# A Mamba scan's inputs: from VectorE and GpSimd to TensorE, with a diagonal that GpSimd selects

## The chip, the cores and the metric

The kernel runs on one core of one Trainium2 chip. The time is that of one launch in microseconds (us) on the device; times of several launches are given by their median. The profile is of one execution; its span runs from the first to the last instruction.

## The reference, cut to what matters

The whole program is four layers, each with an attention-like part and a feed-forward part. The change lies in the first layer's Mamba block, in its scan over time. The input is one sequence of 2048 tokens with 128 features; the block works on 256 channels and 16 states. The kernel takes the tokens in 4 blocks of 512 and the channels as 2 halves (j) of 128 partitions.

```python
dt = softplus(dt_r @ W_dt + b_dt)
A = -exp(A_log)
def step(h, ins):                       # over the 2048 tokens
    dt_t, B_t, C_t, u_t = ins
    dA = exp(dt_t[..., None] * A)
    h = h * dA + (dt_t * u_t)[..., None] * B_t[:, None, :]
    y = einsum('bds,bs->bd', h, C_t)
    return h, y
y = ys + uc * Dskip
```

For one state s, the scan over 512 tokens of a channel needs the factors exp(dt A[s]), the inputs (dt u) B[s], and then h C[s] is summed over s.

## The kernel before, in words

The scan is 64 steps, written out by hand. Step n has token block n // 16 and state n % 16. In each step:

- ScalarE makes the factors (`forget`, L586), one activation for each half j. They go to a PSUM bank (`decay(n, j)`, four banks, chosen by the parity of n and by j) or, in a step of kind T, to one of two SBUF buffers (`kept`).
- Some engine makes the inputs (dt u) B[s]. The string `KIND` says which, one letter for each step.
  - P: GpSimd multiplies `DTU` by a row of B that a DMA has spread over the partitions (`input_of`, L721), into `h(n)`.
  - D: TensorE spreads the row of B into PSUM (`spread`, L381) and VectorE multiplies (L840).
  - T: `DTU` was turned once for each block (`turn_dtu`, L406, kept by ScalarE, L597). Now tokens are the partitions and B[s] is a scalar for each partition, so ScalarE weights the turned copy with four activations (`weight`, L607, into `buT`), and TensorE turns it back into the `decay` bank with eight transposes (`turn_input`, L415).
- VectorE scans each half (`scan`, L860, 128x512), in place into `h(n)`, one of a ring of 5 buffers.
- GpSimd multiplies `h(n)` by the spread row of C (`read_out`, L731, 128x1024) into `hc`, a ring of 3.
- TensorE adds `hc` into the sum y with eight transposing matmuls (`add_y`, L435).

The order on each engine is a loop over n. TensorE issues the input of step n + 2, then now and then `turn_dtu`, `spread` or `turn_gated`, then `add_y(n - 1)`. ScalarE issues `weight(n + 3)`, then `forget(n + 2)`. GpSimd issues `read_out(n)`, then `input_of(n + 3)`. VectorE issues the two scans and, between them or behind them, what else it has. An input of step n by TensorE has to wait until the scan of step n - 2 has read the bank.

The step sizes dt of blocks 2 and 3 are finished during the scan of block 0. ScalarE computes exponentials at n = 1 and 4 and the logarithms at n = 8 (with its tables loaded anew, L566 and L586). VectorE then does `power_series` (L816), `soften` (L821), `add_soft` (L826: `DT` += the logarithm's part) and `scaled_u` (L830: `DTU` = `DT` u). At n = 2, 18, 34 and so on (from the second block on) it also gates the finished block (`gate`, L872, two instructions). At the start of each block `add_y` adds the diagonal of Dskip as well, with sixteen float32 matmuls that are no transposes (L428).

Before: 39 steps of kind T, 20 of kind P, 5 of kind D.

## Time and profile before

| what | us |
|---|---|
| median of 3 runs | 662.57 |
| lowest and highest of them | 659.83, 668.09 |
| the profiled execution, span | 632.2 |
| VectorE busy in it | 452.7 |
| TensorE (matmul) busy in it | 537.4 |
| ScalarE busy in it | 393.8 |
| GpSimd busy in it | 377.5 |
| the scan: start of its first instruction on VectorE, end of its last scan | 66.4, 250.0 |

For the profiled execution the span is what is recorded; a launch's time also holds what lies before and behind the span, and the median is 30.4 us above it. In the profile PE is TensorE's matmuls, PEld its weight loads, DVE VectorE, ACT ScalarE, POOL GpSimd, and L860 is line 860 of the kernel.

### The profile page before, as it was taken

What the parts mean: (1) busy time and instruction counts of PE and PEld (TensorE: products, weight loads), DVE (VectorE), ACT (ScalarE), POOL (GpSimd) and SP (SyncE); (2) the same over time, 40 slices, a digit from 0 to 9 for tenths busy, and PEclk for the clock granted to TensorE, in tenths of its full rate; (3) what the DMA queues carried; (4) which work ended last, traced back from release to release, by engine and by line L of the source; (5) the groups of instructions that cost most, each with busy time, mean ns of one, the idle gap of its engine ahead of it and who ended that gap; (6) DMA issues with size and microseconds to landing.
All of it is one profiled execution on the core that took longest, in us unless ns stands there. A gap on an engine that the chain in (4) does not pass through costs nothing. (4 is left out here: it accounts for less than half of the span.)

```text
span 632.2 us, 10057 instructions
## 1 busy us (share of the span) xinstructions
PE 537.4 (85%) x3490; PEld 423.8 (67%) x3490; DVE 452.7 (72%) x801; ACT 393.8 (62%) x779; POOL 377.5 (60%) x296
## 2 busy tenths in 40 slices
PE   5999867587787878798787989698999988989997
PEld 2444556466675767576654867698788986775766
DVE  6799799999999998898385597153333575658662
ACT  3679899769979987455469496413221135748670
POOL 0588798989999996488540650772900771125430
PEclk9999788799899899999999799899999999999999
DMA  5036053345666640200070000610611210000002
GB/s 131 4 84 108 16 122 101 83 113 130 134 139 131 135 121 2 76 0 2 17 210 3 1 8 28 147 64 17 183 32 45 66 34 2 2 0 1 2 0 67
DMA packets 45819, 40.44 MB, mean 64 GB/s; under 512 B 12183, under 2 KB 32585, under 8 KB 45770
## 3 DMA queue, kind: packets, MB, share of 16 engines
q1 hardware_dynamic: 44746, 37.71, 25.2%
q0 software_dynamic: 1024, 2.10, 1.1%
q8 instruction: 28, 0.46, 0.3%
q14 instruction: 21, 0.17, 0.1%
HBM read 33.70 MB, written 6.09 MB: 63 GB/s over the span
## 5 line engine op out<-in xcount | busy, mean ns | idle before, releaser
L435 PE MATMUL bank<-all_ident,l0s_ring 128*128 128x128 f32 x512 | 72.9, 291 | 18.7 <-POOL l0s_ring L731 18.5
L435 PEld LDWEIGHTS bank<-all_ident,l0s_ring 128*128 128x128 f32 x512 | 61.8, 150 | 27.4 <-POOL l0s_ring L731 24.8
L860 DVE TENSOR_TENSOR_SCAN l0s_ring<-l_XM,l0s_ring,bank 128x512 f32<-128x512 f32 x62 | 74.6, 1254 | 1.8 <-PE bank L415 1.8
L731 POOL TENSOR_TENSOR l0s_ring<-l0s_ring,l0s_c_rest 128x1024 f32<-128x1024 f32 x32 | 66.3, 2092 | 7.9 <-DVE l0s_ring L860 3.6
L731 POOL TENSOR_TENSOR l0s_ring<-l0s_ring,all_XF 128x1024 f32<-128x1024 f32 x31 | 66.2, 2154 | 5.8 <-DVE l0s_ring L860 2.7
L415 PE MATMUL bank<-all_ident,all_XNT 128*128 128x128 f32 x312 | 50.0, 302 | 22.9 <-DVE l0s_ring L860 15.7
L607 ACT ACTIVATE all_XNT<-l_wraw,l_wins 128x256 f32<-128x256 f32 x156 | 66.1, 497 | 0.5 <-PE bank L415 0.4
L860 DVE TENSOR_TENSOR_SCAN l0s_ring<-bank,l0s_ring 128x512 f32<-128x512 f32 x50 | 60.2, 1244 | 5.1 <-ACT bank L586 2.5
L415 PEld LDWEIGHTS bank<-all_ident,all_XNT 128*128 128x128 f32 x312 | 39.3, 156 | 29.7 <-ACT all_XNT L607 12.7
L586 ACT ACTIVATE l_XM<-l_DT,l_negA 128x512 f32<-128x512 f32 x78 | 50.8, 712 | 0.6 <-DVE l0s_ring L860 0.6
L721 POOL TENSOR_TENSOR l0s_ring<-l_DTU,l0s_b_all 128x1024 f32<-128x1024 f32 x20 | 40.1, 2005 | 0.0
L586 ACT ACTIVATE bank<-l_DT,l_negA 128x512 f32<-128x512 f32 x50 | 32.7, 679 | 7.0 <-DVE l0s_ring L860 7.0
L2015 POOL DMA_INDIRECT all_XNT<-gy,all_slot x16 | 15.6, 974 | 35.9 <-DMA gy<-l1s_ys 31.6
L329 PE MATMUL bank<-l_XM,l_wins 128*128 128x512 f32 x64 | 30.9, 627 | 0.9 <-ACT l_XM L530 0.9
L1386 POOL TENSOR_TENSOR l1m_prep<-l1at_NWT,l1at_level 128x512 f32<-128x512 f32 x12 | 15.9, 1351 | 22.8 <-issue 20.5
L2027 POOL TENSOR_TENSOR l1s_xlo<-all_XF,l1s_xhi 128x512 fp32r<-128x512 f32 x7 | 7.7, 1094 | 32.4 <-ACT l1s_xhi L2474 32.4
L2887 PEld LDWEIGHTS bank<-l_w,l_wall 128*128 128x128 f32 x128 | 19.0, 226 | 8.5 <-issue 5.7
L2448 ACT ACTIVATE l1s_U<-bank 128x128 f32<-128x128 f32 x16 | 4.4, 277 | 32.4 <-PE bank L2108 32.4
L329 PEld LDWEIGHTS bank<-l_XM,l_wins 128*128 128x128 f32 x64 | 12.1, 200 | 16.8 <-issue 15.5
L2327 PE MATMUL bank<-all_wdT,l1s_work 128*128 128x128 f32 x192 | 22.8, 275 | 0.0
L2887 PE MATMUL bank<-l_w,l_wall 128*128 128x128 f32 x128 | 19.8, 315 | 3.3 <-ACT l_wall L2895 2.0
L2676 DVE SCALAR_TENSOR_TENSOR l1s_work<-bank,l_wall 128x512 f32<-128x512 f32 x24 | 15.9, 683 | 9.2 <-ACT l_wall L2480 7.3
(442 smaller groups left out, 1497.7 us busy)
## 6 DMA issues: line engine op xcount, KB each, us to landing
l0s_c_rest<-bc_rows SPq DMA_DIRECT2D x16, 512.0 KB, 5.4
all_XF<-bc_rows SPq DMA_DIRECT2D x16, 512.0 KB, 5.3
l0s_b_all<-bc_rows SPq DMA_DIRECT2D x20, 256.0 KB, 6.0
l_wall<-in_L_ffn_W SPq DMA_DIRECT2D x14, 256.0 KB, 4.7
all_X<-in_L_attn_x SPq DMA_DIRECT2D x4, 256.0 KB, 3.5
gx<-l1m_TD SPq DMA_DIRECT2D x1, 1024.0 KB, 5.6
gy<-l1m_TD SPq DMA_DIRECT2D x1, 1024.0 KB, 8.6
out<-all_X SPq DMA_DIRECT2D x4, 256.0 KB, 2.3
```

The lines of the kernel that those rows point to most:

```text
L329: last = nc.tensor.matmul(S.bank[j][:, :], wins[:, k, j * P:(j + 1) * P], XM[:, b * BLK + k:b * BLK + k + BLK], start=(k == 0), stop=(k == ...
L415: last = nc.tensor.transpose(decay(n, j)[:, bass.ts(k, P)], buT[i % 2][:, k, j * P:(j + 1) * P], S.ident[:, :])
L435: last = nc.tensor.matmul(y_of(k, j), hc[n % CRING][:, j, bass.ts(k, P)], S.ident[:, :], start=False, stop=(n % DS == DS - 1 and k % 2 == ...
L586: nc.scalar.activation(dst, DT[:, j, block_of(n)], ACT.Exp, scale=negA[:, j, n % DS:n % DS + 1]).then_inc(decay_ready, 1)
L607: last = nc.scalar.activation(buT[i % 2][:, k, :], dtuT[:, k, :], ACT.Identity, scale=bT[:, n // DS * TPB + k, DR + n % DS:DR + n % DS + 1])
L721: nc.gpsimd.tensor_tensor(h(n)[:, :, :], DTU[:, :, block_of(n)], wide(b_wide[i % HRING]), ALU.mult).then_inc(bu_pool, 1)
L731: nc.gpsimd.tensor_tensor(hc[n % CRING][:, :, :], h(n)[:, :, :], wide(c_wide[p % HRING][:, n % 2, :]), ALU.mult).then_inc(hc_ready, 1)
L860: nc.vector.tensor_tensor_scan(h(n)[:, j, :], factor, added, before, ALU.mult, ALU.add).then_inc(h_ready, 1)
L1386: nc.gpsimd.tensor_tensor(LL[:, LEVELS - 1 - l, q, :, :], LT[:, quads(q), :], quad(level[:, l, :]), ALU.mult).then_inc(ll_ready, 1)
L2327: last = nc.tensor.matmul(out_bank[:, bass.ts(k, P)], hid[b % 2][:, f, bass.ts(k, P)], wdT[:, f, :], start=(b >= NBLK and f == 0 and k == ...
L2676: nc.vector.scalar_tensor_tensor(hid[b % 2][:, f, :], up_bank[n][:, :], QSCALE, sg[n % 2], ALU.mult, ALU.mult).then_inc(hid_done, 1)
L2887: last = self.nc.tensor.matmul(out, self.hid[b % 2][:, f, bass.ts(k, P)], self.E.down(0)[:, f, :], start=(f == 0), stop=(f == FE - 1))
```

## The change

- There is a new kind of step, G. GpSimd makes a diagonal matrix of B[s] for each of a block's four tiles of 128 tokens in one instruction (`diagonal`, an affine select on 128x512 that keeps the element where column equals partition and writes zero elsewhere), and TensorE multiplies the turned dt u by it (`spread_input`, eight float32 matmuls of 128x128 that are no transposes). This turns back and weights at once, and ScalarE has nothing to weight. 26 steps are G, 34 T, 2 P and 2 D.
- Both kinds keep their factors in the two `kept` buffers, so `forget(n)` of all steps from the fourth on waits for the scan of step n - 2.
- The turned dt u has two buffers, chosen by the block's parity, the second in `OUTF`, whose first use there (`q_of[2]`) must be over: `keep_dtu(1)` waits for `dt_ready` 3.
- `add_soft` and `scaled_u` of blocks 2 and 3 move from VectorE to GpSimd, one step earlier in the loop: behind `read_out` at n = 10 and 13, and n = 11 and 14.

The diff, without the lines that declare the semaphore `diag_ready`:

```diff
--- before.py
+++ after.py
@@ -184,9 +184,11 @@
         STEPS = NBLK * DS
         EXP_AT, LOG_AT = (1, 4), 8
         TURN_AT, ROWS_AT = (4, 6), (STEPS - 7, STEPS - 5, STEPS - 3, STEPS - 1)
-        KIND = "DPDPTPTTPTTPTTPT" + (NBLK - 2) * "PTTPTTPTDTPTTPTT" + "PTTPTTPTDTPTTTTT"
+        KIND = "DPDPTGGTGGTGTTTT" + "TTGTGTGTGTTGTGTG" + 2 * "TGTGTTGTGTGTTGTG"
         LAST = STEPS - 1
         number = lambda n: KIND[:n].count(KIND[n])
+        by_pe = [n for n in range(STEPS) if KIND[n] in "TG"]
+        turns = lambda n: sum(m < n for m in by_pe)
         BC = DR + DS
         GROUP = [slice(0, TPB), slice(TPB, TILES)]
         with Phase(nc, "l0s") as ph:
@@ -215,8 +217,9 @@
 
             buT = [S.XNT[:, i * 2 * TPB:(i + 1) * 2 * TPB, :].rearrange("p (k j) d -> p k (j d)", j=JT) for i in range(2)]
             kept = [XM[:, i * W2:(i + 1) * W2].rearrange("p (j t) -> p j t", j=JT) for i in range(2)]
-            dtuT = wraw[:, 0:W2].rearrange("p (k c) -> p k c", k=TPB)
+            dtuT = [v[:, 0:W2].rearrange("p (k c) -> p k c", k=TPB) for v in (wraw, S.OUTF)]
             bT = wins[:, :, :].rearrange("p k d -> p (k d)")[:, 0:TILES * BC].rearrange("p (n c) -> p n c", c=BC)
+            diagB = [v.rearrange("p (k t) -> p k t", k=TPB) for v in (win[:, :], wins[:, :, :].rearrange("p k d -> p (k d)")[:, BLK:2 * BLK])]
             nw = (6 * P + FF0) // Q16
             wa, wc = (ring[:, PADS + 3 * SPOT + i * nw * Q16:PADS + 3 * SPOT + (i + 1) * nw * Q16].rearrange("p (n q) -> p n q", q=Q16) for i in range(2))
             nq = TPB * P // Q16
@@ -413,6 +416,17 @@
                             pe.wait_ge(h_ready, JT * (n - 2) + j + 1)
                             for k in range(TPB):
                                 last = nc.tensor.transpose(decay(n, j)[:, bass.ts(k, P)], buT[i % 2][:, k, j * P:(j + 1) * P], S.ident[:, :])
+                            last.then_inc(bu_turned, 1)
+
+                    def spread_input(n):
+                        i = number(n)
+                        pe.wait_ge(diag_ready, i + 1)
+                        pe.wait_ge(dtu_kept, 2 * (n // DS + 1))
+                        for j in range(JT):
+                            pe.wait_ge(h_ready, JT * (n - 2) + j + 1)
+                            for k in range(TPB):
+                                last = nc.tensor.matmul(decay(n, j)[:, bass.ts(k, P)], dtuT[n // DS % 2][:, k, j * P:(j + 1) * P], diagB[i % 2][:, k, :],
+                                                        start=True, stop=True)
                             last.then_inc(bu_turned, 1)
 
                     def add_y(n):
@@ -488,6 +502,8 @@
                     for n in range(STEPS + 1):
                         if n + 2 < STEPS and KIND[n + 2] == "T":
                             turn_input(n + 2)
+                        if n + 2 < STEPS and KIND[n + 2] == "G":
+                            spread_input(n + 2)
                         if n + 6 < STEPS and (n + 6) % DS == 0:
                             turn_dtu((n + 6) // DS, 0)
                             turn_dtu((n + 6) // DS, 1)
@@ -574,15 +590,15 @@
                             nc.scalar.activation(wdT[0:96, 2, :], S.bank[5][0:96, 2 * P:3 * P], ACT.Copy).then_inc(w_copied, 1)
 
                     def forget(n, j):
-                        if KIND[n] == "T":
-                            i = number(n)
+                        if KIND[n] in "TG":
+                            i = turns(n)
                             if i >= 2:
-                                act.wait_ge(h_ready, JT * [m for m in range(n) if KIND[m] == "T"][i - 2] + j + 1)
+                                act.wait_ge(h_ready, JT * by_pe[i - 2] + j + 1)
                         elif n >= 2:
                             act.wait_ge(h_ready, JT * (n - 2) + j + 1)
                         if n % DS == 0 and j == 0:
                             act.wait_ge(dt_ready, n // DS + 1)
-                        dst = kept[number(n) % 2][:, j, :] if KIND[n] == "T" else decay(n, j)[:, :]
+                        dst = kept[turns(n) % 2][:, j, :] if KIND[n] in "TG" else decay(n, j)[:, :]
                         nc.scalar.activation(dst, DT[:, j, block_of(n)], ACT.Exp, scale=negA[:, j, n % DS:n % DS + 1]).then_inc(decay_ready, 1)
 
                     def keep_b():
@@ -590,21 +606,23 @@
                         nc.scalar.activation(bT, bank_t[:, 0:TILES * BC].rearrange("p (n c) -> p n c", c=BC), ACT.Copy).then_inc(b_kept, 1)
 
                     def keep_dtu(b):
-                        if b:
-                            act.wait_ge(weighted, KIND[:b * DS].count("T"))
+                        if b == 1:
+                            act.wait_ge(dt_ready, 3)
+                        elif b:
+                            act.wait_ge(bu_turned, JT * turns((b - 1) * DS))
                         for i in range(2):
                             act.wait_ge(dtu_turned, 2 * b + i + 1)
-                            nc.scalar.activation(dtuT[:, 2 * i:2 * i + 2, :], (bank_b if i else bank_t)[:, :].rearrange("p (k c) -> p k c", k=2),
+                            nc.scalar.activation(dtuT[b % 2][:, 2 * i:2 * i + 2, :], (bank_b if i else bank_t)[:, :].rearrange("p (k c) -> p k c", k=2),
                                                  ACT.Copy).then_inc(dtu_kept, 1)
 
                     def weight(n):
                         i = number(n)
                         if i >= 2:
-                            act.wait_ge(bu_turned, JT * (i - 1))
+                            act.wait_ge(bu_turned, JT * (turns([m for m in by_pe if KIND[m] == "T"][i - 2]) + 1))
                         act.wait_ge(b_kept, 1)
                         act.wait_ge(dtu_kept, 2 * (n // DS + 1))
                         for k in range(TPB):
-                            last = nc.scalar.activation(buT[i % 2][:, k, :], dtuT[:, k, :], ACT.Identity,
+                            last = nc.scalar.activation(buT[i % 2][:, k, :], dtuT[n // DS % 2][:, k, :], ACT.Identity,
                                                         scale=bT[:, n // DS * TPB + k, DR + n % DS:DR + n % DS + 1])
                         last.then_inc(weighted, 1)
 
@@ -730,6 +748,26 @@
                             pool.wait_ge(y_added, n - CRING + 1)
                         nc.gpsimd.tensor_tensor(hc[n % CRING][:, :, :], h(n)[:, :, :], wide(c_wide[p % HRING][:, n % 2, :]), ALU.mult).then_inc(hc_ready, 1)
 
+                    def diagonal(n):
+                        i = number(n)
+                        pool.wait_ge(b_kept, 1)
+                        if i >= 2:
+                            pool.wait_ge(bu_turned, JT * (turns([m for m in by_pe if KIND[m] == "G"][i - 2]) + 1))
+                        else:
+                            pool.wait_ge(z_ready, 2 * NBLK)
+                        row = bT[:, n // DS * TPB:(n // DS + 1) * TPB, DR + n % DS:DR + n % DS + 1]
+                        nc.gpsimd.affine_select(out=diagB[i % 2], in_=row.broadcast_to([P, TPB, P]), compare_op=ALU.is_equal, fill=0.0, base=0,
+                                                pattern=[[0, TPB], [1, P]], channel_multiplier=-1).then_inc(diag_ready, 1)
+
+                    def add_soft(b):
+                        pool.wait_ge(softened, b + 1)
+                        pool.wait_ge(max_ready, JT * (b + 1))
+                        nc.gpsimd.tensor_tensor(DT[:, :, blk(b)], DT[:, :, blk(b)], q_of[b], ALU.add).then_inc(dt_ready, 1)
+
+                    def scaled_late(b):
+                        pool.wait_ge(dt_ready, b + 1)
+                        nc.gpsimd.tensor_tensor(DTU[:, :, blk(b)], DT[:, :, blk(b)], UC[:, :, blk(b)], ALU.mult).then_inc(dtu_late, 1)
+
                     nc.gpsimd.memset(wraw[96:P, 2 * P:3 * P], 0.0).then_inc(zeroed, 1)
                     nc.gpsimd.memset(wraw[96:P, 5 * P:6 * P], 0.0).then_inc(zeroed, 1)
                     pool.wait_ge(zeroed, 2)
@@ -759,6 +797,12 @@
                             read_out(n)
                         if n + 3 < STEPS and KIND[n + 3] == "P":
                             input_of(n + 3)
+                        if n + 3 < STEPS and KIND[n + 3] == "G":
+                            diagonal(n + 3)
+                        if n in (10, 13):
+                            add_soft(2 if n == 10 else 3)
+                        if n in (11, 14):
+                            scaled_late(2 if n == 11 else 3)
 
                 @block.vector
                 def _(dve):
@@ -825,10 +869,6 @@
                         dve.wait_ge(max_ready, JT * (b + 1))
                         nc.vector.tensor_tensor(DT[:, :, blk(b)], DT[:, :, blk(b)], q_of[b], ALU.add).then_inc(dt_ready, 1)
 
-                    def scaled_u(b):
-                        dve.wait_ge(dt_ready, b + 1)
-                        nc.vector.tensor_tensor(DTU[:, :, blk(b)], DT[:, :, blk(b)], UC[:, :, blk(b)], ALU.mult).then_inc(dtu_late, 1)
-
                     def input_of(n):
                         dve.wait_ge(b_spread, number(n) + 1)
                         if n // DS < 2:
@@ -846,7 +886,7 @@
                         elif KIND[n] == "D":
                             dve.wait_ge(bu_dve, i + 1)
                         else:
-                            dve.wait_ge(bu_turned, JT * i + j + 1)
+                            dve.wait_ge(bu_turned, JT * turns(n) + j + 1)
                             if n == 4:
                                 dve.wait_ge(wq_ready, 1)
                             if n >= RING:
@@ -855,8 +895,8 @@
                         if n >= DS:
                             dve.wait_ge(h_ready, JT * (n - DS) + j + 1)
                         before = h(n - DS)[:, j, BLK - 1:BLK] if n >= DS else 0.0
-                        factor = kept[i % 2][:, j, :] if KIND[n] == "T" else decay(n, j)[:, :]
-                        added = decay(n, j)[:, :] if KIND[n] == "T" else h(n)[:, j, :]
+                        factor = kept[turns(n) % 2][:, j, :] if KIND[n] in "TG" else decay(n, j)[:, :]
+                        added = decay(n, j)[:, :] if KIND[n] in "TG" else h(n)[:, j, :]
                         nc.vector.tensor_tensor_scan(h(n)[:, j, :], factor, added, before, ALU.mult, ALU.add).then_inc(h_ready, 1)
 
                     def read_last():
@@ -922,10 +962,6 @@
                             power_series(2 if n == 3 else 3)
                         if n in (10, 13):
                             soften(2 if n == 10 else 3)
-                        if n in (11, 14):
-                            add_soft(2 if n == 11 else 3)
-                        if n in (12, 15):
-                            scaled_u(2 if n == 12 else 3)
                         if n >= DS and n % DS == 2:
                             gate(n // DS - 1)
                     read_last()
```

## Rows read from the trace of the kernel before

**Rows 1.** The page: the span, and VectorE's busy tenths in 40 slices

```profile
span 632.2 us, 10057 instructions
...
DVE  6799799999999998898385597153333575658662
```

**Rows 2.** Windows, one for each quarter of the scan: busy us (instructions) of each engine, clock, DMA

```profile
66.30:124.96 58.66, 39.74 (x240) 34.09 (x240) 54.79 (x45) 53.31 (x96) 50.16 (x23) 0.79 0.35 86
124.96:166.19 41.23, 32.36 (x243) 27.50 (x241) 40.22 (x37) 34.93 (x71) 39.28 (x21) 0.96 0.54 123
166.19:207.56 41.37, 32.40 (x243) 27.95 (x242) 40.17 (x36) 37.83 (x77) 41.13 (x22) 0.96 0.64 134
207.56:250.00 42.44, 34.14 (x262) 30.07 (x262) 40.38 (x35) 36.25 (x73) 39.29 (x20) 0.96 0.39 87
```

**Rows 3.** Groups by line and shape, VectorE, 66 to 254 us: busy, mean ns | idle before

```profile
L860 DVE TENSOR_TENSOR_SCAN l0s_ring<-l_XM,l0s_ring,bank 128x512 f32<-128x512 f32 x62 | 74.6, 1254 | 1.8 <-PE bank L415 1.8
L860 DVE TENSOR_TENSOR_SCAN l0s_ring<-bank,l0s_ring 128x512 f32<-128x512 f32 x50 | 60.2, 1244 | 5.1 <-ACT bank L586 2.5 <-POOL l0s_ring L721 2.4
L860 DVE TENSOR_TENSOR_SCAN l0s_ring<-l_XM,bank 128x512 f32<-128x512 f32 x16 | 18.4, 1196 | 0.4 <-ACT l_XM L586 0.4
L840 DVE TENSOR_TENSOR l0s_ring<-l_DTU,bank 128x1024 f32<-128x1024 f32 x5 | 6.0, 1200 | 3.0 <-PE bank L381 3.0
...
L830 DVE TENSOR_TENSOR l_DTU<-l_DT,l_UC 128x1024 f32<-128x1024 f32 x2 | 3.9, 1965 | 0.0
L826 DVE TENSOR_TENSOR l_DT<-l_DT,all_OUTF 128x1024 f32<-128x1024 f32 x2 | 3.9, 1964 | 0.0
```

**Rows 4.** Timeline of VectorE: start, us, instructions, idle before and its releaser

```profile
105.07 2.34 DVE L860 TENSOR_TENSOR_SCAN l0s_ring<-bank,l0s_ring 128x512 f32<-128x512 f32 x2 [1.55 <-ACT bank L586]
107.33 1.20 DVE L826 TENSOR_TENSOR l_DT<-l_DT,all_OUTF 128x1024 f32<-128x1024 f32 x1
...
118.95 2.73 DVE L826 TENSOR_TENSOR l_DT<-l_DT,all_OUTF 128x1024 f32<-128x1024 f32 x1
...
127.33 4.76 DVE L860 TENSOR_TENSOR_SCAN l0s_ring<-l_XM,l0s_ring,bank 128x512 f32<-128x512 f32 x4
132.01 1.25 DVE L872 TENSOR_TENSOR l_ZT<-bank,l_ZT 128x512 f32<-128x512 f32 x2
...
239.09 2.45 DVE L860 TENSOR_TENSOR_SCAN l0s_ring<-l_XM,l0s_ring,bank 128x512 f32<-128x512 f32 x2 [0.55 <-PE bank L415]
```

**Rows 5.** Timeline of GpSimd in the scan

```profile
63.14 2.35 POOL L708 TENSOR_TENSOR l_DTU<-l_DT,l_UC 128x1024 f32<-128x1024 f32 x1
...
90.80 2.98 POOL L731 TENSOR_TENSOR l0s_ring<-l0s_ring,all_XF 128x1024 f32<-128x1024 f32 x1
...
233.21 7.88 POOL L731 TENSOR_TENSOR l0s_ring<-l0s_ring,l0s_c_rest 128x1024 f32<-128x1024 f32 x4
```

**Rows 6.** Timeline of GpSimd in the next layer, where it selects on 128x512

```profile
361.83 0.63 POOL L1381 TENSOR_SCALAR_AFFINE_SELECT l1at_DEC<-l1at_DEC 128x512 f32<-128x512 f32 x1 [2.02 <-ACT l1at_DEC L1606]
...
364.85 1.05 POOL L1381 TENSOR_SCALAR_AFFINE_SELECT l1at_DEC<-l1at_DEC 128x512 f32<-128x512 f32 x1 [1.37 <-ACT l1at_DEC L1606]
```

**Rows 7.** Timeline of TensorE: two stretches of the scan

```profile
133.32 2.05 PE L428 MATMUL bank<-l_diagD,l_UC 128*128 128x128 f32 x16 [0.52 <-DVE l_ZT L872]
135.21 1.91 PE L435 MATMUL bank<-all_ident,l0s_ring 128*128 128x128 f32 x16
```

**Rows 8.** Timeline of TensorE in a stretch at the lower clock

```profile
85.49 1.82 PE L435 MATMUL bank<-all_ident,l0s_ring 128*128 128x128 f32 x8
```

**Rows 9.** Window of that stretch

```profile
83.70:87.10 3.40, 3.40 (x16) 3.17 (x17) 3.05 (x3) 3.40 (x8) 2.66 (x3) 0.50 0.29 98
```

**Rows 10.** Timeline of ScalarE behind its two logarithms

```profile
102.98 1.28 ACT L586 ACT_TABLE_LOAD   x1
...
105.52 1.69 ACT L607 ACTIVATE all_XNT<-l_wraw,l_wins 128x256 f32<-128x256 f32 x4
107.12 2.54 ACT L586 ACTIVATE l_XM<-l_DT,l_negA 128x512 f32<-128x512 f32 x4
```

4 lines of the change are left out of this document (2 added, 2 removed).

## The prediction

> **What bounds the kernel now.** I read the page first, for where VectorE's tenths stay at nines [rows 1]: from slice 4 to 15, the scan. Then the windows over its four blocks [rows 2]. VectorE is busy 54.8 of 58.7 us in the first, and 40.2, 40.2 and 40.4 of 41.2, 41.4 and 42.4 in the others. GpSimd comes close behind it (50.2, 39.3, 41.1, 39.3), ScalarE and TensorE lie lower. Scans are serial on VectorE: 128 of them at 1.20 to 1.25 us [rows 3]. So VectorE's queue is the path, and what counts is what leaves it and what can't keep up with it afterwards. The groups by line [rows 3] show both at once: busy time of each thing that VectorE does, and its idle time with the releaser. Beyond the scan nothing reads what the change moves, so a gain there passes to the end undiminished.
>
> Back to back, four scans take 4.68 us (start 127.33 to the gate at 132.01) [rows 4], 1.17 each, 2.34 a step; the gate takes 1.2. A block of 16 steps thus costs VectorE 37.4 + 1.2 = 38.7 us at least, against the 41.2 to 42.4 that it takes now. In the first block, whose scans start from zero (mean 1196 ns, not 1254 [rows 3]), I take 1.12 a scan and 2.24 a step.
>
> **What leaves VectorE.** Three of five D inputs at 1.20 (L840), two `add_soft` at 1.96 and two `scaled_u` at 1.97 [rows 3]: 3.6 + 3.9 + 3.9 = 11.4 us, all on the path. With them go two kinds of waits: for GpSimd's inputs (L721), 2.4 us, and for TensorE's turned inputs (L415), 1.8 us [rows 3]. The latter stand where KIND ends in five T steps: a T step costs ScalarE four weights and two factors, and its scans start late (0.55 idle at 239.09 [rows 4]). The new string has no such run at its end. Upper bound: 15.6 us.
>
> The moved operations are worth their means because of how they collide. `add_soft` took 1.20 us once and 2.73 the other time [rows 4], and a `read_out` beside such an operation took 2.98 in place of 1.97 [rows 5]. Both engines lose when VectorE has two operands in SBUF. A scan has one in SBUF and one in PSUM, so it doesn't disturb GpSimd. The Trainium skill, SBUF — State Buffer, "Who interferes with whom", states this as an exclusive lock on a shared port pair that a VectorE instruction with two SBUF inputs takes against a GpSimd instruction that reads SBUF. The trace agrees (2.73 against 1.20). By this rule no other sum comes out, but it says that the moved pair costs GpSimd no collision of its own.
>
> **What comes on GpSimd.** A `read_out` costs 1.97 (four in 7.88 [rows 5]), and so does an input. A moved operation costs 2.3, by its twin of the early blocks, 2.35 [rows 5]. The diagonal is not in the scan before. The next layer has the same instruction on the same shape: 0.63, or 1.05 beside VectorE instructions of another kind [rows 6]. The input here is a broadcast column, which no row shows for a select. I take 0.63, since only scans run beside it, and keep 1.05 for the range. A block behind the first has 16 read-outs and 7 diagonals: 31.5 + 4.4 = 35.9 us (38.9 by the high price) against VectorE's 38.7. GpSimd has room, or just none.
>
> A diagonal can also be late rather than too much. `diagonal(n + 3)` stands behind `read_out(n)`, which starts when scan n ends. 1.97 + 0.63, then four matmuls and their latency, 0.65: 3.3 us. The scan that needs it starts four scans later, 4.7. Slack 1.4 us (1.0 by the high price), so GpSimd may trail by about one microsecond before VectorE waits.
>
> At the end of the first block it trails by more. I count from the end of ScalarE's table load at 104.3 behind the logarithms [rows 10]. Scan 11 can end 2.9 later (half its factors 0.62, two scans). From there GpSimd has five read-outs (9.8), one of them stretched by 1.0 beside `soften`, and three of the moved operations (6.9), then the diagonal of step 18 (0.6) and the matmuls (0.65): 21.9 in all. VectorE would be at scan 18 at 20.6 (next paragraph). Cost 1.3 us, once; then GpSimd catches up 2.8 us a block.
>
> **What comes on ScalarE.** Five weights of 1.6 us fewer in all, so less work. But steps 12 to 17 are now all T, which makes 1.6 + 1.24 = 2.84 a step on ScalarE [rows 10] against 2.24 on VectorE; before, P steps stood among them and VectorE's moved work covered them. From the end of the table load: factors of 11 (1.24), five weights (8.0), the turned dt u of block 1 (1.05), factors of 12 to 15 (5.0) and half of 16 (0.6): scan 16 at 15.9. VectorE alone: 0.6 + 5 x 2.24 + 1.9 for `soften` = 13.7. Cost 2.2 us. Scan 16 stands at 124.96 now, 20.7 behind the same mark, so even so it comes 4.8 earlier. After it two T steps at 2.34 make the 20.6 above. The 1.55 us that VectorE waits at 105.07 for these tables [rows 4] shrink little. In later blocks T runs are two long. `keep_gated`, queued ahead of two factors, makes one step late by some 0.4 in each: 1 us for the three with jitter. That all factors now wait for the scan two steps back costs nothing while ScalarE is on time: 3 scans (3.5 us) lie between, for at most 2.84 of work.
>
> **What comes on TensorE.** 39 steps were its own, now 60. Sixteen float32 matmuls that are no transposes take 2.05, sixteen transposes 1.91 [rows 7]: 0.128 and 0.119 each at the full clock. A block: 16 `add_y` 15.3, 9 T 8.6, 7 G 7.2, the Dskip diagonal 2.05, turning dt u and the gated rows 2.9: 36.0 of 38.7 us. It fits, with 7% to spare, so I count nothing; the cover is the 1.4 us of slack. At the lower clock eight take 1.82 [rows 8], where the granted clock is 0.50, 1.2 GHz [rows 9]; a step then takes 3.64, 1.3 over VectorE's. The blocks behind the first had 0.96 on average [rows 2], one short stretch each, in which TensorE had been idle often. It will be idle less, so I expect no more of them.
>
> The Trainium skill speaks against the change here. FP8 and Floating Point Precision, "TensorE Precision Notes", has true float32 take four passes through the array, and TensorE: Matmul & The Clock Gate, "Terms", calls transpose mode four times faster for float32. By that rule each G step would cost four times the transposes' time; the row has 0.128 against 0.119, 8% more, on the same shape and kind of operands. I follow the row.
>
> **DMA.** 18 of 20 spreads of B (256 KB each) go; VectorE never waits for one, so nothing.
>
> **The sum.** 11.4 + 2.4 + 1.8 - 1.3 - 2.2 - 1.0 = 11.1 us off the scan. The profiled span would go from 632.2 to 621.1. What lies around it, 30.4 us between that span and the median of the runs, stays: 662.6 - 11.1 = 651.5, say 651, 1.7% less. A change under 2%, 13 us, is about what a measurement of this kernel can't tell from none.
>
> **The rivals.** (A) GpSimd becomes the second bound: diagonals cost 1.05 or more each, GpSimd needs 38.9 a block, and every run of G T G waits. For it: GpSimd was within 2 us of VectorE before, and a broadcast input is unseen. Against: 0.63 stands for the quiet case. Bound by GpSimd, the three blocks give back 0.2 each, and by late diagonals some 0.3 on 21 G steps: 6 to 7 us lost, 658. (B) The waits that I added don't come: ScalarE and GpSimd have enough run-up before step 12 and 18, since both lose work in the first ten steps. Then 15.6 of gain less 0.6: 647; and if the wait at 105.07 goes too, 645. (C) The other side: TensorE becomes the bound. Non-transposing matmuls in float32, or a busy engine that is stopped by late diagonals, put it at 1.2 GHz for long stretches. At 1.3 us a step it takes 9 such steps to eat the gain and 19 to be slower by 2%; at two of the three blocks, 32 steps, 651 + 42 = 693. By the page's four passes, worked out from the rows: a G step needs 8 x 4 x 0.119 + 0.95 = 4.8, 2.4 over VectorE's, on 26 steps 62 us: 713. Against both: [rows 7], and a clock of 0.96 on average with TensorE busy 32 of 41 us [rows 2]. That the change doesn't do what it says can be seen from the diff only for GpSimd's select, and would be (A).
>
> **How the numbers follow.** Forecast 0.55, with 646 to 656 as its own range; A 0.20; B 0.18; C 0.07 (clock 0.05, four passes 0.02). Forecast and B hold the faster side: all of B, and a third of the forecast's cases end under 649.3. Faster by over 2% 0.35, within 2% 0.58, slower 0.07. The range takes in B's low end, with a few microseconds for the spread of the runs (659.8 to 668.1), and A's high end: 642 to 662.
>
> **What would show it.** In the new profile: scan stage 66.4 to about 239 rather than 250; VectorE's blocks behind the first at 38.7 to 39.5 us; L826 and L830 as GpSimd groups at 2.3 each; selects at 0.63; VectorE's idle in front of scans released by ScalarE at steps 12 to 16, once by TensorE at 18; the L415-like group of G at 0.128 spacing. The prediction is wrong if VectorE waits on TensorE in every G step (A or C), if the granted clock falls under 0.9 behind the first block (C), or if GpSimd's read-outs stretch beside scans.

## The result: faster by 0.8%, less than half of what was forecast

Before 664.28 us (median of 20 runs), after 659.73 (20 runs). The ratio is 0.9922, 95% interval 0.9901 to 0.9944, so about 5 us or 0.8% faster, where 11.1 us were forecast. The direction is right; the size is not.

The traces need one remark. The first trace of before has a span of 632.2 us, 30 us under that kernel's median. A second trace of before (the run `null_before` below) has 664.5, and 31.3 of the 32.3 us between them lie behind the scan. The largest piece that I found is one wait of GpSimd at a phase's end, behind sixteen indirect DMAs: 11.9 us in the first trace, 26.6 in the second:

```profile
459.32 0.20 POOL L2041 MEMSET l1s_ST<- 128x128 f32 x1 [26.57 <-POOLq L63]
```

That run took 666.31 us for a span of 664.5, and after's profiled run 661.33 for 659.6. So only 1.8 us lie around the span, and not the 30.4 that the prediction put there. The record doesn't say which chip the first trace is from; on the chip of the last four experiments this kernel's spans were 632.6 to 641.8 us, so it is most likely one of that kind. The scan itself is nearly the same in both traces of before: 182.4 and 182.8 us from the start of the first scan to the end of the last. All sums below are made inside the scan.

Line numbers are those of each kernel, and they shift. In after L900 is a scan, L912 the gate, L418 the input of a T step, L428 that of a G step (in before L428 was the diagonal of Dskip, now L442), L449 `add_y`, L460 `turn_gated`, L602 a factor, L625 a weight, L632 `keep_gated`, L759 the new diagonal, L765 and L769 the two moved operations.

I cut the scan at the starts of steps 16, 32 and 48 on VectorE, by the starts of single scans in the traces:

| kernel | first block | second | third | fourth | scan, us |
|---|---|---|---|---|---|
| before (second trace) | 57.8 | 41.2 | 41.4 | 42.5 | 182.8 |
| after | 52.7 | 45.3 | 41.1 | 41.4 | 180.5 |
| forecast | 52.5 | 40.4 | 39.1 | 39.1 | about 171 |

The last row isn't in the prediction; I put it together from its parts. Scan 16 was to come 4.8 us earlier (57.3 in the first trace, less 4.8), the later blocks were to take 38.7 to 39.5 us, and 1.3 us of waiting at step 18 falls in the second. The first block came out as forecast, within 0.2 us; how far that was luck, the experiments show. The loss stands in the three others: 4.9, 2.0 and 2.3 us. VectorE's groups in after, to be read against [rows 3]:

```profile
L900 DVE TENSOR_TENSOR_SCAN l0s_ring<-l_XM,l0s_ring,bank 128x512 f32<-128x512 f32 x96 | 114.7, 1258 | 10.4 <-ACT l_XM L602 5.0 <-PE bank L428 3.0 <-PE bank L418 2.1
L900 DVE TENSOR_TENSOR_SCAN l0s_ring<-l_XM,bank 128x512 f32<-128x512 f32 x24 | 27.4, 1197 | 3.6 <-ACT l_XM L602 2.3 <-PE bank L418 1.4
L900 DVE TENSOR_TENSOR_SCAN l0s_ring<-bank,l0s_ring 128x512 f32<-128x512 f32 x8 | 9.3, 1207 | 1.6 <-ACT bank L602 1.5
```

L826 and L830 are gone from this view and L840 (now L880) has 2 instructions left. But the idle time ahead of scans is 15.6 us, where it was 1.8 + 5.1 + 0.4 = 7.3. The timeline of VectorE says where, against [rows 4]. Steps 11, 12, 15, 16 and 17, then 18, then around the gates (L912):

```profile
106.63 2.33 DVE L900 TENSOR_TENSOR_SCAN l0s_ring<-l_XM,bank 128x512 f32<-128x512 f32 x2 [2.25 <-ACT l_XM L602]
109.46 2.33 DVE L900 TENSOR_TENSOR_SCAN l0s_ring<-l_XM,bank 128x512 f32<-128x512 f32 x2 [0.49 <-PE bank L418]
...
119.11 2.33 DVE L900 TENSOR_TENSOR_SCAN l0s_ring<-l_XM,bank 128x512 f32<-128x512 f32 x2 [0.41 <-PE bank L418]
122.01 4.79 DVE L900 TENSOR_TENSOR_SCAN l0s_ring<-l_XM,l0s_ring,bank 128x512 f32<-128x512 f32 x4 [0.56 <-PE bank L418]
129.63 2.65 DVE L900 TENSOR_TENSOR_SCAN l0s_ring<-l_XM,l0s_ring,bank 128x512 f32<-128x512 f32 x2 [2.83 <-PE bank L428]
132.20 1.26 DVE L912 TENSOR_TENSOR l_ZT<-bank,l_ZT 128x512 f32<-128x512 f32 x2
...
144.78 2.45 DVE L900 TENSOR_TENSOR_SCAN l0s_ring<-l_XM,l0s_ring,bank 128x512 f32<-128x512 f32 x2 [1.16 <-ACT l_XM L602]
147.60 2.45 DVE L900 TENSOR_TENSOR_SCAN l0s_ring<-l_XM,l0s_ring,bank 128x512 f32<-128x512 f32 x2 [0.36 <-ACT l_XM L602]
150.91 23.54 DVE L900 TENSOR_TENSOR_SCAN l0s_ring<-l_XM,l0s_ring,bank 128x512 f32<-128x512 f32 x20 [0.85 <-PE bank L418]
174.37 1.25 DVE L912 TENSOR_TENSOR l_ZT<-bank,l_ZT 128x512 f32<-128x512 f32 x2
...
186.23 2.45 DVE L900 TENSOR_TENSOR_SCAN l0s_ring<-l_XM,l0s_ring,bank 128x512 f32<-128x512 f32 x2 [1.16 <-ACT l_XM L602]
189.05 7.30 DVE L900 TENSOR_TENSOR_SCAN l0s_ring<-l_XM,l0s_ring,bank 128x512 f32<-128x512 f32 x6 [0.37 <-ACT l_XM L602]
...
215.49 1.26 DVE L912 TENSOR_TENSOR l_ZT<-bank,l_ZT 128x512 f32<-128x512 f32 x2
```

These lines show three kinds of wait. At 106 the 2.25 is for ScalarE's factors behind its logarithms. From 109 to 122 the waits of 0.49 (twice), 0.41 and 0.56 come from ScalarE's run of T steps: they name TensorE, but TensorE itself had been waiting for ScalarE's weights (L625), as its line for step 15 shows:

```profile
118.42 1.09 PE L418 MATMUL bank<-all_ident,all_XNT 128*128 128x128 f32 x8 [1.90 <-ACT all_XNT L625]
```

At 129.63 step 18 waits 2.83 for TensorE's new line L428. Behind the gates a scan waits 1.16 for a factor of ScalarE, twelve microseconds after the gate, and the next one 0.37; this repeats at 186.23 and, not shown, at 227.35. From gate to gate it is 42.2 and 41.1 us.

GpSimd's new groups in after:

```profile
L759 POOL TENSOR_SCALAR_AFFINE_SELECT l_wins<-l_wins 128x512 f32<-128x512 f32 x13 | 9.3, 714 | 0.0
L759 POOL TENSOR_SCALAR_AFFINE_SELECT l_win<-l_wins 128x512 f32<-128x512 f32 x13 | 8.3, 638 | 0.0
L769 POOL TENSOR_TENSOR l_DTU<-l_DT,l_UC 128x1024 f32<-128x1024 f32 x2 | 4.7, 2364 | 0.0
L765 POOL TENSOR_TENSOR l_DT<-l_DT,all_OUTF 128x1024 f32<-128x1024 f32 x2 | 4.7, 2358 | 0.0
```

The select costs 0.64 (one took 1.62, beside a VectorE operation with two SBUF inputs), a moved operation 2.36. These prices were forecast well, 0.63 and 2.3. The select that step 18 needs comes late all the same, since it stands behind a read-out:

```profile
124.87 2.00 POOL L749 TENSOR_TENSOR l0s_ring<-l0s_ring,all_XF 128x1024 f32<-128x1024 f32 x1
126.82 0.64 POOL L759 TENSOR_SCALAR_AFFINE_SELECT l_wins<-l_wins 128x512 f32<-128x512 f32 x1
```

TensorE's prices were not forecast well. Its timeline in after at the first late diagonal and in the third block:

```profile
127.52 3.44 PE L428 MATMUL bank<-l_wins,all_OUTF 128*128 128x128 f32 x16 [3.77 <-POOL l_wins L759]
130.80 1.04 PE L449 MATMUL bank<-all_ident,l0s_ring 128*128 128x128 f32 x8
...
132.54 1.95 PE L428 MATMUL bank<-l_win,all_OUTF 128*128 128x128 f32 x16
```

```profile
183.31 1.04 PE L449 MATMUL bank<-all_ident,l0s_ring 128*128 128x128 f32 x8
184.18 0.60 PE L460 MATMUL bank<-all_ident,l_ZT 128*128 128x128 f32 x4
...
186.37 1.95 PE L428 MATMUL bank<-l_wins,l_wraw 128*128 128x128 f32 x16
```

A G step issues 16 MATMULs for its 8 calls, and takes 1.95 us, not 1.03. And the windows, one around the first line of that timeline and then the last three blocks, with the columns of [rows 2]:

```profile
127.50:130.90 3.40, 3.38 (x17) 3.38 (x18) 1.27 (x1) 1.78 (x5) 3.40 (x2) 0.56 0.77 137
...
122.00:167.30 45.30, 39.74 (x337) 38.31 (x335) 39.43 (x34) 36.42 (x72) 38.83 (x26) 0.96 0.34 89
167.40:208.40 41.00, 39.66 (x345) 37.90 (x344) 39.05 (x35) 36.30 (x73) 35.81 (x24) 1.00 0.46 103
208.50:249.80 41.30, 39.91 (x348) 38.20 (x347) 39.27 (x35) 33.39 (x65) 35.76 (x23) 1.00 0.33 73
```

TensorE is busy 39.7 of 41.0 us in the third block, where it was 32.4 of 41.4. It looks like the bound. Whether it is, the experiments had to say.

### The profile page after: what moved, and what is told of

Its sections match the earlier page's. It is cut to its first block and busy times, and to the rows that moved or that the text cites. A ratio compares the mean times of both kernels' runs of the same rounds, so it can differ in the third digit from the quotient of the medians.

```text
span 659.6 us, 10816 instructions
## 1 busy us (share of the span) xinstructions
PE 575.4 (87%) x3860; PEld 465.6 (71%) x3860; DVE 447.1 (68%) x794; ACT 386.9 (59%) x759; POOL 365.9 (55%) x308
## 5 line engine op out<-in xcount | busy, mean ns | idle before, releaser
L900 DVE TENSOR_TENSOR_SCAN l0s_ring<-l_XM,l0s_ring,bank 128x512 f32<-128x512 f32 x96 | 114.7, 1258 | 10.4 <-ACT l_XM L602 5.0
L602 ACT ACTIVATE l_XM<-l_DT,l_negA 128x512 f32<-128x512 f32 x120 | 79.1, 712 | 8.8 <-DVE l0s_ring L900 8.8
L449 PE MATMUL bank<-all_ident,l0s_ring 128*128 128x128 f32 x512 | 66.0, 273 | 0.3 <-POOL l0s_ring L749 0.3
L449 PEld LDWEIGHTS bank<-all_ident,l0s_ring 128*128 128x128 f32 x512 | 57.8, 141 | 0.7 <-POOL l0s_ring L749 0.7
L418 PE MATMUL bank<-all_ident,all_XNT 128*128 128x128 f32 x272 | 35.6, 274 | 6.1 <-ACT all_XNT L625 6.1
L418 PEld LDWEIGHTS bank<-all_ident,all_XNT 128*128 128x128 f32 x272 | 30.4, 141 | 7.6 <-ACT all_XNT L625 7.5
L2051 POOL DMA_INDIRECT all_XNT<-gy,all_slot x16 | 15.6, 976 | 35.5 <-DMA gy<-l1s_ys 31.2
L625 ACT ACTIVATE all_XNT<-all_OUTF,l_wins 128x256 f32<-128x256 f32 x72 | 30.5, 496 | 0.2
L900 DVE TENSOR_TENSOR_SCAN l0s_ring<-l_XM,bank 128x512 f32<-128x512 f32 x24 | 27.4, 1197 | 3.6 <-ACT l_XM L602 2.3
L2484 ACT ACTIVATE l1s_U<-bank 128x128 f32<-128x128 f32 x16 | 4.4, 277 | 40.5 <-PE bank L2144 32.1
L625 ACT ACTIVATE all_XNT<-l_wraw,l_wins 128x256 f32<-128x256 f32 x64 | 27.1, 496 | 0.2
L1607 PE MATMUL bank<-l1m_TD,l1m_prep 128*128 128x128 f32 x96 | 15.6, 320 | 13.1 <-DVE l1m_TD L1934 7.7
L1607 PEld LDWEIGHTS bank<-l1m_TD,l1m_prep 128*128 128x128 f32 x96 | 14.1, 228 | 14.3 <-issue 10.2
```

The source lines that it names most:

```text
L418: last = nc.tensor.transpose(decay(n, j)[:, bass.ts(k, P)], buT[i % 2][:, k, j * P:(j + 1) * P], S.ident[:, :])
L449: last = nc.tensor.matmul(y_of(k, j), hc[n % CRING][:, j, bass.ts(k, P)], S.ident[:, :], start=False, stop=(n % DS == DS - 1 and k % 2 == ...
L602: nc.scalar.activation(dst, DT[:, j, block_of(n)], ACT.Exp, scale=negA[:, j, n % DS:n % DS + 1]).then_inc(decay_ready, 1)
L625: last = nc.scalar.activation(buT[i % 2][:, k, :], dtuT[n // DS % 2][:, k, :], ACT.Identity, scale=bT[:, n // DS * TPB + k, DR + n % DS:DR ...
L900: nc.vector.tensor_tensor_scan(h(n)[:, j, :], factor, added, before, ALU.mult, ALU.add).then_inc(h_ready, 1)
L1607: last = nc.tensor.matmul(S.bank[2 * q][:, bass.ts(k, P)], LL[:, LEVELS - 1 - l, q, k, :], TD[:, q * TPB + k, :], start=True, stop=True)
```

## The experiments

Three theories. (1) TensorE's load: a G step costs nearly twice what I thought, and a block needs about 38.7 us of TensorE (an estimate from its lines), as much as of VectorE. (2) Late diagonals: their place behind `read_out` in GpSimd's queue. (3) The hand-over. After each gate TensorE turns the gated rows (`turn_gated`, L460) and ScalarE copies them out of the bank (`keep_gated`, L632). ScalarE works its queue in order, so while `keep_gated` waits for `turn_gated`, the two factors behind it wait too. Beside them the question what each half of the change does alone.

Ratios are to before on the same chip. The last four experiments, from first_gate on, ran on a chip where before takes 639.16 us, not 664. No trace of before was kept there; the first trace of before, which is as short, has a scan of 182.4 us, the second 182.8. `null_before` is before once more.

**null_before.** 

> The kernel before once more, for its spread and for a second trace. Ratio to before 1.000 with an interval of about 0.003 to either side. Its scan should again take 183 to 184 us on VectorE from its first input to its last scan; the time behind the scan is expected near 405 us, as in the trace of after, and not the 382 us of the first trace of before.

Ratio 0.9996 (0.9963 to 1.0028). Scan 182.8, behind it 413 us, 31 more than in the first trace. So differences of ratios under 0.003 mean nothing, and the blocks of the scan are the finer measure. Between the two traces of before the first block differs by 0.5 us, the others by 0.01, so 0.5 us of any whole scan below can be chance; each of the other kernels has but one trace.

**g_one_pass.** Theory 1 by itself: G's product in half the MATMULs. It leaves out the factor B of these steps, so only its time counts.

```diff
 for k in range(TPB):
-    last = nc.tensor.matmul(decay(n, j)[...], dtuT[n // DS % 2][...], diagB[i % 2][:, k, :], start=True, stop=True)
+    last = nc.tensor.transpose(decay(n, j)[...], dtuT[n // DS % 2][...], S.ident[:, :])
```

> After, with each G step's product done as eight transposes against the identity in place of eight float32 matmuls against the diagonal, which is still selected and waited for. The input of these steps is left without its factor B, so the output is another one. Theory 1 (TensorE is the second bound: in the trace of after a G step issues 16 MATMULs, two for each call, and costs 1.8 us, not 1.0, so that a block needs 38.7 us of TensorE, as much as of VectorE): a G step falls to 0.9 us, a block to 32.5 us of TensorE, the waits of VectorE behind each gate (0.3 to 1.2 us each, 1.5 to 2 us a block) mostly go, and the time falls by 4 to 6 us against after, ratio to before 0.984 to 0.987. Theory 2 (late diagonals and order on GpSimd): nothing but the wait at step 18 matters and it stays, within 1 us of after, ratio 0.991 to 0.994. Theory 3 (the hand-over of the gated rows from TensorE to ScalarE waits for its place in the order, whatever TensorE's load is): within 1.5 us of after.

Ratio 0.9906 (0.9872 to 0.9939). The ratio can't tell it from after, the scan can: 175.0, with blocks 52.1, 43.0, 39.9, 40.0. It is 5.5 us shorter than after, 5.0 without the first block. The wait at 18 is 1.9 in place of 2.8, the waits behind the gate of the third block 0.27 and 0.37 in place of 1.16 and 0.37. Theory 1 forecast 4 to 6 us and gets them in the scan, though not in the ratio (it had 0.984 to 0.987). But the larger waits only shrank, at the same steps; two small ones (0.34 and 0.22 at steps 21 and 22) went.

**diag_first.** Theory 2: the order on GpSimd.

```diff
 for n in range(STEPS):
+    if n + 3 < STEPS and KIND[n + 3] == "G":
+        diagonal(n + 3)
     if n < LAST:
         read_out(n)
-    if n + 3 < STEPS and KIND[n + 3] == "G":
-        diagonal(n + 3)
```

> After, with diagonal(n + 3) issued ahead of read_out(n) on GpSimd, not behind it. Theory 1 (TensorE): the 2.8 us wait of VectorE at step 18 shrinks to 1 us or less, since TensorE turns the input while GpSimd reads out, the waits behind the gates stay; 1 to 2.5 us faster than after, ratio 0.988 to 0.991. Theory 2 (late diagonals): the waits behind the gates go as well, 4 to 6 us faster than after, ratio 0.984 to 0.987. Theory 3: as theory 1.

Ratio 0.9839 (0.9785 to 0.9893). Scan 176.4, blocks 52.5, 42.5, 40.7, 40.8; 4.1 us off after, 2.8 of them in the second block. From step 16, which it waits for, VectorE goes through step 18 without a stop, up to the gate:

```profile
120.73 7.20 DVE L900 TENSOR_TENSOR_SCAN l0s_ring<-l_XM,l0s_ring,bank 128x512 f32<-128x512 f32 x6 [0.57 <-PE bank L418]
127.84 1.26 DVE L912 TENSOR_TENSOR l_ZT<-bank,l_ZT 128x512 f32<-128x512 f32 x2
```

TensorE's product of step 18 starts 3.55 us behind scan 16 and takes 2.05. In after it started 5.51 behind it, later by one read-out of 2.00, and took 3.44: TensorE had idled for 3.77 us, and the clock granted there was 0.56, near the lower of its two levels (the window above). So the late diagonal had been paid twice, once for the select's place and once for the clock. The waits behind the gates stayed (0.76 and 0.37 in the third block): theory 2 is a part, not the whole.

**inputs_only.** The change without the moved step sizes.

```diff
 # vector
 if n in (10, 13):
     soften(2 if n == 10 else 3)
+if n in (11, 14):
+    add_soft(2 if n == 11 else 3)
+if n in (12, 15):
+    scaled_u(2 if n == 12 else 3)
 # gpsimd
-if n in (10, 13):
-    add_soft(2 if n == 10 else 3)
-if n in (11, 14):
-    scaled_late(2 if n == 11 else 3)
```

> After, with add_soft and scaled_u of blocks 2 and 3 back on VectorE in their old places: the G and T inputs alone. Theory 1 (TensorE bounds the blocks behind the first): VectorE reaches step 16 some 4 us later, GpSimd is not behind then and the wait at step 18 (2.8 us) goes; later blocks stay at 41 us; 1 to 3 us slower than after, ratio 0.995 to 1.000. Rival (the moved step sizes carry the whole gain at 7.8 us of VectorE's queue): 5 us slower or more, ratio 1.000 or above.

Ratio 0.9888 (0.9844 to 0.9931). Scan 178.6, blocks 53.6, 42.5, 41.15, 41.4. Neither expectation: both had it slower than after, and its scan is 1.9 us shorter. Three of the four moved operations, back on VectorE in this kernel:

```profile
107.78 1.20 DVE L857 TENSOR_TENSOR l_DT<-l_DT,all_OUTF 128x1024 f32<-128x1024 f32 x1
111.14 1.20 DVE L861 TENSOR_TENSOR l_DTU<-l_DT,l_UC 128x1024 f32<-128x1024 f32 x1
117.85 1.20 DVE L857 TENSOR_TENSOR l_DT<-l_DT,all_OUTF 128x1024 f32<-128x1024 f32 x1
```

All four take 1.20, 4.8 us together, where before they took 1.20, 2.74, 2.73 and 1.20, 7.9 together. With GpSimd's P inputs gone, each of them starts ahead of GpSimd's read-out, which then takes 2.84 in place of 2.00; in before two of them started behind an instruction of GpSimd and took the longer time themselves. So 3.1 of the 7.8 us are saved by the new inputs, whether anything is moved or not; VectorE's other operations with two SBUF inputs in that block fall from 9.9 us (7.6 in the first trace of before, which waits 1.7 us more) to 7.1. That is how this kernel has 4.2 of the 5.1 us that after gains in the first block. Of the 4.8 us that the move takes off VectorE, 1.95 come back in after as the four waits for ScalarE's run of T steps, and 0.7 as a longer `soften` (1.93 for 1.20, beside a read-out): over steps 11 to 15, where the two kernels differ on VectorE, this kernel is only 1.4 us longer, over the whole first block 1.0. And the second block, where GpSimd isn't behind now, is 2.9 shorter.

**steps_only.** The other half alone: before with `add_soft` and `scaled_u` moved.

```diff
 # vector
-if n in (11, 14):
-    add_soft(2 if n == 11 else 3)
-if n in (12, 15):
-    scaled_u(2 if n == 12 else 3)
 # gpsimd
+if n in (10, 13):
+    add_soft(2 if n == 10 else 3)
+if n in (11, 14):
+    scaled_late(2 if n == 11 else 3)
```

> Before, with only add_soft and scaled_u of blocks 2 and 3 moved to GpSimd, as in after. Scan of before, first scan to last: 57.8 + 41.2 + 41.4 + 42.5 = 182.8 us by block. Theory A (moved steps pay what they took on VectorE): the first block falls by 5 to 7 us, the others stay, scan 176 to 178. Theory B (they only move the load from the first engine to the second, GpSimd, which then has 44 + 9 us against VectorE's 49): the first block falls by 3 to 5, the second rises by 1 to 3, scan 179 to 182.

Ratio 0.9992 (0.9970 to 1.0015): nothing. Scan 185.2, 2.4 longer than before: the first block 2.7 shorter, the second 4.8 longer. Both theories had a gain. B is right in its direction, the first block's gain taken back in the second, but the second loses more than it allowed (1 to 3), so that nothing is left. VectorE in the trace of this kernel, steps 16 and 18:

```profile
123.70 2.46 DVE L873 TENSOR_TENSOR_SCAN l0s_ring<-bank,l0s_ring 128x512 f32<-128x512 f32 x2 [3.64 <-POOL l0s_ring L721]
...
130.85 2.45 DVE L873 TENSOR_TENSOR_SCAN l0s_ring<-l_XM,l0s_ring,bank 128x512 f32<-128x512 f32 x2 [2.34 <-PE bank L415]
```

VectorE waits 3.64 us for GpSimd's input of step 16, which stands behind `scaled_u` and two read-outs, then 2.34 for a turned input.

**first_steps_dve.** diag_first and inputs_only together.

```diff
 # gpsimd
+if n + 3 < STEPS and KIND[n + 3] == "G":
+    diagonal(n + 3)
 if n < LAST:
     read_out(n)
-if n + 3 < STEPS and KIND[n + 3] == "G":
-    diagonal(n + 3)
-if n in (10, 13):
-    add_soft(2 if n == 10 else 3)
-if n in (11, 14):
-    scaled_late(2 if n == 11 else 3)
 # vector
+if n in (11, 14):
+    add_soft(2 if n == 11 else 3)
+if n in (12, 15):
+    scaled_u(2 if n == 12 else 3)
```

> Diagonals ahead of the read-outs and the late step sizes back on VectorE. If the moved steps cost 1.9 us in after (scan 180.5 against 178.6 without them) only because diagonals came late behind them, they are worth their first-block gain here: this scan is 0.5 to 1.5 us longer than that of diag_first, 177 to 178. Rival (they cost on their own, by GpSimd's lag): it is as short or shorter, 175 to 176.4.

Ratio 0.9830 (0.9798 to 0.9863). Scan 176.5, blocks 54.1, 41.0, 40.65, 40.75, against 176.4 for diag_first. With the moved operations back on VectorE the first block is 1.6 longer and the second 1.5 shorter. The result, 0.1 longer, lies between the two expectations (0.5 or more, or as short): even with diagonals first the moved operations are worth nothing.

**gate_later.** Theory 3: the hand-over, on after as it is.

```diff
-TURN_AT, ROWS_AT = (4, 6), ...
+TURN_AT, ROWS_AT = (4, 7), ...
 # scalar
-if n > DS and n % DS - 1 in TURN_AT:
-    keep_gated(n // DS - 1, TURN_AT.index(n % DS - 1))
+if n > DS and n % DS - 2 in TURN_AT:
+    keep_gated(n // DS - 1, TURN_AT.index(n % DS - 2))
```

> After, with ScalarE's keep_gated one step later (n % 16 = 6 and 9) and TensorE's second turn_gated one step later (n % 16 = 7), so that ScalarE does not wait at the head of its queue while two factors stand behind it. If the order of the hand-over makes the waits of 1.16 and 0.37 us behind each gate, blocks three and four fall from 41.1 and 41.4 to 39.5 to 40.0 and the scan to 176 to 177.5. If TensorE's load behind the gate makes them (it has no idle for 15 us there), the waits move to the scans that wait for TensorE and the blocks stay at 40.5 or more, scan 179 to 180.5.

Ratio 0.9829 (0.9799 to 0.9859). Scan 174.5, blocks 52.1, 43.1, 39.06, 40.3: 6.0 us off after (5.4 without the first block, which the edit doesn't touch), by moving three numbers, with the same work on every engine. That is more than the expectation had for theory 3 (176 to 177.5). This decides between theories 1 and 3 for the third block: all seven G steps are in it, TensorE does what it did, and the block takes 39.06, where theory 1 had 40.5 or more. Timeline of VectorE in it, gate to gate:

```profile
170.79 1.26 DVE L912 TENSOR_TENSOR l_ZT<-bank,l_ZT 128x512 f32<-128x512 f32 x2
171.97 9.54 DVE L900 TENSOR_TENSOR_SCAN l0s_ring<-l_XM,l0s_ring,bank 128x512 f32<-128x512 f32 x8
181.69 28.25 DVE L900 TENSOR_TENSOR_SCAN l0s_ring<-l_XM,l0s_ring,bank 128x512 f32<-128x512 f32 x24 [0.19 <-PE bank L418]
209.86 1.27 DVE L912 TENSOR_TENSOR l_ZT<-bank,l_ZT 128x512 f32<-128x512 f32 x2
```

ScalarE's `keep_gated` (L632) in after, and in this kernel:

```profile
184.82 0.60 ACT L632 ACTIVATE l_DTU<-bank 128x512 f32<-128x512 f32 x1 [3.26 <-PE bank L460]
185.31 1.32 ACT L602 ACTIVATE l_XM<-l_DT,l_negA 128x512 f32<-128x512 f32 x2
```

```profile
181.36 0.58 ACT L632 ACTIVATE l_DTU<-bank 128x512 f32<-128x512 f32 x1
181.84 1.94 ACT L602 ACTIVATE l_XM<-l_DT,l_negA 128x512 f32<-128x512 f32 x3
```

In after there are 3.26 us of waiting in front of `keep_gated`, and the factors stand behind it; in this kernel there is none.

**balanced.** Diagonals first, the later hand-over, step 14 G instead of T, and P for one G of each later block.

```diff
-KIND = "DPDPTGGTGGTGTTTT" + "TTGTGTGTGTTGTGTG" + 2 * "TGTGTTGTGTGTTGTG"
+KIND = "DPDPTGGTGGTGTGTT" + "TTGTGTGTGTTPTGTG" + 2 * "TGTPTTGTGTGTTGTG"
```

> Diagonals first, the later hand-over, and another KIND: step 14 is G in place of T (the run of T on ScalarE is broken), and one G of each later block is P (at 27, 35, 51), which takes 1.8 us from TensorE and gives 1.3 to GpSimd. If TensorE, ScalarE and GpSimd are the second bounds one behind the other, each of these gives 0.5 to 2: first block 50 to 51.5, second 40 to 41, others 39.3 to 40, scan 169 to 172.5, ratio to before 0.97 to 0.98. If the order alone matters and not the load, no better than diag_first with the later hand-over: scan 173 to 175, ratio 0.98.

Ratio 0.9813 (0.9774 to 0.9853). Scan 172.7, blocks 50.2, 42.4, 40.2, 39.8. The first block improves as expected, the others don't, and the scan lies between what the two expectations had (169 to 172.5, 173 to 175, nearer the first). Only with first_gate beside it can this be read.

**first_gate.** Both orders mended, KIND as in after.

```diff
-TURN_AT, ROWS_AT = (4, 6), ...
+TURN_AT, ROWS_AT = (4, 7), ...
 # scalar
-if n > DS and n % DS - 1 in TURN_AT:
-    keep_gated(n // DS - 1, TURN_AT.index(n % DS - 1))
+if n > DS and n % DS - 2 in TURN_AT:
+    keep_gated(n // DS - 1, TURN_AT.index(n % DS - 2))
 # gpsimd
+if n + 3 < STEPS and KIND[n + 3] == "G":
+    diagonal(n + 3)
 if n < LAST:
     read_out(n)
-if n + 3 < STEPS and KIND[n + 3] == "G":
-    diagonal(n + 3)
```

> After with both changes of order: diagonals ahead of the read-outs, and the later hand-over of the gated rows. If the two waits are separate, their gains add: scan 180.5 - 4.1 - 6.0 = 170.4 us, 170 to 172, blocks behind the second at 39.0 to 39.5, ratio to before 0.975 to 0.980. If they are one lag seen twice, 173 to 174.5.

Ratio 0.9766 (0.9734 to 0.9798), the lowest of all, though the interval overlaps those of the three variants that follow. Scan 170.9, blocks 52.3, 40.1, 38.68, 39.8: the gains add (9.6 us off after, for 4.1 and 6.0). The third block is VectorE's own sum, 38.7, from gate to gate:

```profile
128.28 1.26 DVE L912 TENSOR_TENSOR l_ZT<-bank,l_ZT 128x512 f32<-128x512 f32 x2
129.46 4.79 DVE L900 TENSOR_TENSOR_SCAN l0s_ring<-l_XM,l0s_ring,bank 128x512 f32<-128x512 f32 x4
135.30 33.08 DVE L900 TENSOR_TENSOR_SCAN l0s_ring<-l_XM,l0s_ring,bank 128x512 f32<-128x512 f32 x28 [1.05 <-PE bank L418]
168.30 1.26 DVE L912 TENSOR_TENSOR l_ZT<-bank,l_ZT 128x512 f32<-128x512 f32 x2
169.48 37.59 DVE L900 TENSOR_TENSOR_SCAN l0s_ring<-l_XM,l0s_ring,bank 128x512 f32<-128x512 f32 x32
206.98 1.27 DVE L912 TENSOR_TENSOR l_ZT<-bank,l_ZT 128x512 f32<-128x512 f32 x2
208.16 21.19 DVE L900 TENSOR_TENSOR_SCAN l0s_ring<-l_XM,l0s_ring,bank 128x512 f32<-128x512 f32 x18
229.82 2.45 DVE L900 TENSOR_TENSOR_SCAN l0s_ring<-l_XM,l0s_ring,bank 128x512 f32<-128x512 f32 x2 [0.47 <-ACT l_XM L602]
```

These are 32 scans in 37.59 us without a wait. Balanced's third block is 1.5 longer (a wait of 1.25 at step 37, for a turned input, two steps behind its P step): TensorE didn't need the relief there. Which part of the P step makes that wait, no run separates.

**first_gate_one_pass.** Is TensorE's load still worth anything? To first_gate, in G's product (again without the factor B):

```diff
-last = nc.tensor.matmul(decay(n, j)[...], dtuT[n // DS % 2][...], diagB[i % 2][:, k, :], start=True, stop=True)
+last = nc.tensor.transpose(decay(n, j)[...], dtuT[n // DS % 2][...], S.ident[:, :])
```

> The same as first_gate with each G step's product as eight transposes against the identity (the inputs of these steps are left without their factor B). TensorE's load falls from about 38.7 to 32.4 us a block. If the load still costs something with both orders mended, the scan is 1 us or more shorter than that of first_gate; if the order was all, within 0.5 us, and blocks three and four stay at 39.0 to 39.5, VectorE's own sum.

Ratio 0.9783 (0.9735 to 0.9830), not to be told from first_gate. Scan 169.5, 1.4 shorter: 1.1 of it in the last block, where two late waits for ScalarE go, the rest in the first two, within the spread. The third stays at 38.68. So the load, worth 5.5 us in the order of after, is worth 1.4 once the order is mended.

**first_gate_dve.** And the moved operations? To first_gate:

```diff
 # vector
+if n in (11, 14):
+    add_soft(2 if n == 11 else 3)
+if n in (12, 15):
+    scaled_u(2 if n == 12 else 3)
 # gpsimd
-if n in (10, 13):
-    add_soft(2 if n == 10 else 3)
-if n in (11, 14):
-    scaled_late(2 if n == 11 else 3)
```

> The same with add_soft and scaled_u of blocks 2 and 3 on VectorE. The moved steps cost 1.9 us in after and 0.1 to 0.3 with diagonals first; if they are worth nothing because ScalarE's run of T steps hides them on VectorE and GpSimd's lag takes back the rest, this scan is within 0.7 us of first_gate. If they pay once both orders are mended, it is 1 to 1.6 us longer (the first block's difference).

Ratio 0.9776 (0.9739 to 0.9813). Scan 170.7 against 170.9: blocks 53.5 and 38.7 for the first two, where first_gate has 52.3 and 40.1. Worth nothing here too.

**kind_only.** Step 14 as G on top of first_gate.

```diff
-KIND = "DPDPTGGTGGTGTTTT" + "TTGTGTGTGTTGTGTG" + 2 * "TGTGTTGTGTGTTGTG"
+KIND = "DPDPTGGTGGTGTGTT" + "TTGTGTGTGTTGTGTG" + 2 * "TGTGTTGTGTGTTGTG"
```

> The same as first_gate with step 14 as G in place of T and nothing else. If ScalarE's run of T steps costs what the trace of after shows (waits of 0.49, 0.49, 0.41 and 0.56 us behind the logarithms), the first block falls by 1.2 to 2 us and, unless the diagonal of step 18 takes it back as in the kernel balanced (1.6 us of wait there), the scan by as much: 168.5 to 170. If it is taken back, 170 to 171.5.

Ratio 0.9798 (0.9746 to 0.9850). Scan 170.9, blocks 50.3 and 42.1. The first block gains 2.0, the second loses 2.0, in a wait of 2.5 us at step 18 for TensorE's product (L428). In this trace GpSimd selects the diagonal of step 18 at 124.29, straight behind the last of its moved operations, as at 124.03 in first_gate; only VectorE is there sooner. What lets VectorE out of the first block earlier meets GpSimd still at its moved operations. The obvious next kernel, step 14 as G with these operations left on VectorE, wasn't run.

## Why the prediction was wrong, point by point

Two steps of it failed. It took the moved operations' 7.8 us as all on the path, and they are worth nothing. And it gave the two hand-overs between queues, the late diagonal and `keep_gated`, 1.3 and 1.0 us, and they cost 4.1 and about 6 (9.6 together). The terms of its sum, with what the runs showed:

- **VectorE's queue is the path, and a block can take 38.7 us.** Right: 38.68 in the third block of first_gate. The forecast of 171 for the scan is met by first_gate (170.9), but that is partly luck: first_gate_dve, in which nothing is moved, has 170.7. What the move was to bring came from elsewhere, in part from collisions that the new inputs end.
- **"The moved operations are worth their means", 7.8 us "all on the path".** The first step that failed. In the order of after they are worth -1.9 (178.6 without them, 180.5 with them), alone -2.4, with diagonals first 0.1, with both orders mended -0.3. Three things were missed. Of the 7.8, 3.1 were waits of VectorE for GpSimd inside these instructions, which go with the P inputs: left on VectorE they take 4.8. ScalarE's run of T steps then hides part of the rest, so that putting them back costs the first block 1.0 to 1.6. I had set that run against them at 2.2, which left 5.6. And on GpSimd their 9.4 us make it late for the next block, which takes back what the first gave.
- **The diagonal of step 18, 1.3 us.** Mis-sized: 2.83 in the trace. Diagonals first takes 2.8 off this block and 4.1 off the scan. The missing part is in TensorE's answer: 0.65 was put for four matmuls at the full clock. The scan started 2.11 us behind TensorE's first MATMUL, and the 16 took 3.44 at a granted 0.56.
- **`keep_gated`, 0.4 a block and 1.0 with jitter.** Mis-sized: 1.16 and 0.37 in each block, and 0.85 more at step 25 in the second; the later hand-over is worth 6.0 us. I counted ScalarE's own work there and let TensorE's `turn_gated` come on time. It stands behind `add_y(n - 1)`, which stands behind the 16 MATMULs of the Dskip diagonal, two `add_y` that the gate held up, and now 1.95 us for each G. Before, the same wait was there (8.1 us of ScalarE's time in three places, 10.9 in five in after), and no scan waited behind it.
- **TensorE, 36.0 us a block.** Wrong by a misreading: the 16 MATMULs of 2.05 us in [rows 7] are 8 calls of the code, also where the text ahead of the prediction speaks of sixteen. So a call costs about twice a transposing one, not 8% more. A G step is 1.95, and the same sum gives about 42 a block; the sum counts each group's latency as well, and in the third block of first_gate TensorE is busy 38.2 of 38.7 us. Yet it was no bound: that block takes VectorE's own 38.68 with all seven G steps in it, if with half a microsecond to spare. TensorE's load acts through the hand-over: half the MATMULs are worth 5.5 us in the order of after and 1.4 in that of first_gate.
- **ScalarE's run of T, 2.2 us.** Right: 1.95 in four waits; one T less gives 2.0 in the first block.
- **The first block.** 52.5 forecast, 52.7 measured, and by luck: 4.2 of the 5.1 us gained there come with the inputs alone, which the sum gave nothing for in this block. The sum and the count of ScalarE's queue also differ: 7.8 less 2.2 is 5.6, where scan 16 was put 4.8 earlier.

Of the rivals, A (GpSimd's prices) didn't come: 0.64 a select. B (the added waits stay away) didn't either: they all came. C's mechanism, TensorE near its bound, was half there, at 5.5 us in place of 42 or 62, and not by the clock: 0.96 to 1.00 behind step 18. None of the prediction's own signs of being wrong appeared either: no wait in every G step, no granted clock under 0.9 over a block behind the first, read-outs of 2.00 beside scans. They watched each engine's load, and the loss lay in the order.

The page's four passes (the Trainium skill, FP8 and Floating Point Precision, "TensorE Precision Notes") were turned into four times a transposing product. That isn't what the trace shows: two MATMULs a call, 1.95 us against 1.04 for a transposing step, a factor of 1.9. How many passes one of these MATMULs makes, no row shows. But a rule that spoke for more than one pass was a reason to count the MATMULs against the calls before the row was followed.

**What stays open.** The whole time fell by more than the scan in every kernel but g_one_pass: after 5.2 us against 2.3, diag_first 10.7 against 6.5, first_gate 15.0 against 11.9, steps_only 0.5 against a scan 2.4 longer; g_one_pass 6.2 against 7.8. The stretch behind the scan was 403 to 413 us long in the traces on the slower chips, without an order that follows the changes. No run separates these 3 us or so from the spread of single traces. And the wait at step 11, behind the logarithms, 2.25 to 2.47 us, is left in every kernel with G steps; no run here takes it up.

## What to carry to other kernels

When an engine at its limit is relieved, follow each in-order queue that feeds it past the next hand-over, not just its sum of work: here two misplaced instructions (a select behind a read-out, a copy ahead of two factors) held back 10 us that the loads allowed. Work taken off the busiest engine is worth little where that engine would wait anyway, and it can be worth less than nothing on an engine whose delay reaches the next stage; try each half of a change alone. An instruction's mean can hold waiting for another engine: look at its shortest time before you count on the mean. Count a group's instructions against the calls in the code before its duration is divided by them.

## What the runs showed of the hardware that I had not expected

A float32 matmul of 128x128 that is no transpose is two MATMULs of 0.11 us each, by their spacing (16 for 8 calls in 1.95 us), a transposing one is one (8 in 1.04). A select on GpSimd with a broadcast input costs what one without costs, 0.64 against 0.63 us on 128x512, beside scans that read one operand from SBUF. A VectorE `tensor_tensor` of 128x1024 with both inputs in SBUF took 1.20 us where it started ahead of GpSimd's read-out, which then took 2.84 in place of 2.00, and 2.74 where GpSimd had started first. One and the same kernel takes 25 us less on one chip than on others (639 and 664 us); between the two traces of before 15 of 32 us are in one wait behind indirect DMAs.
